# Moving the copy of the transposed attention output from ScalarE to VectorE

## The chip, the cores and the metric

The program runs on one Trainium2 chip, on all 8 of its NeuronCores, one launch for everything. Each core takes half of the query rows of one of four batch entries. The cores exchange nothing. The metric is the device time of the slowest core, in microseconds (us). Engines are named as in the profile: PE is TensorE's matmul, PEld its weight load, DVE is VectorE, ACT is ScalarE, POOL is GpSimd, SP is SyncE.

## The reference

One transformer layer on x of 4 x 2048 x 4096: a layer norm, causal attention with 32 query heads of width 128 that share one key and one value head (with ALiBi position biases), and a quantised linear layer, all added to x.

```python
xn = _layernorm(x, axis=-1)
q = (xn @ Wq).reshape(B, S, 32, 128); kv = xn @ Wkv
k, v = kv[..., :128], kv[..., 128:]
scores = einsum('bqhd,bkd->bhqk', q, k) * 128 ** -0.5 + alibi bias, causal mask
attn = einsum('bhqk,bkd->bqhd', softmax(scores), v)
W = ((w_q - 128).reshape(O, I // 32, 32) * scales[:, :, None]).reshape(O, I)
out = x + attn.reshape(B, S, H) @ Wo + einsum('bsi,oi->bso', xn, W)
```

## The kernel before

The five stages run one after the other on each core.

- Stage A (layer norm): 16 token blocks of 128 are normalised on VectorE and transposed on TensorE; the transposed tiles psA_tr leave PSUM by copies that alternate between ScalarE and VectorE (lines 311 and 316). Keys kt and values vt are computed here.
- Stage B (queries): 64 products of 32 matmuls each (line 411) into qat, which holds 32 heads x 1024 queries, written by ScalarE (line 423).
- Stage C (attention): the stage that the change touches.
- Stage D (output projection): 128 products of 32 matmuls (line 756) that read qat, now the attention output.
- Stage E (quantised layer): dequantisation on VectorE, transposes, matmuls (line 888), sum with x.

**Stage C.** A query pass r (0 or 1) covers 512 queries, and inside a pass the loop runs over the 32 heads. The key blocks (128 keys each) that a head needs are taken in pairs, called groups; the first pass has up to 8 blocks (4 groups), the second up to 16 (8 groups). Blocks whose ALiBi weight is zero are left out, so the first heads have fewer. For one group the work is:

1. two score matmuls of 512 columns into psC_sc (line 524), two slots in PSUM;
2. one exp over 128x1024 on ScalarE into expb (line 551), three slots in SBUF;
3. on VectorE the weights and masks: for heads 0 to 7 ("narrow") small operations per query block (lines 574, 576, 603, some on GpSimd, line 614), for heads 8 to 31 ("wide") only a mask over 128x512 (line 562), and only for four key blocks of the pass: those of groups 0 and 1 in the first pass, of groups 2 and 3 in the second;
4. up to 8 matmuls of 129 columns that multiply with the values into psC_av (line 654). For a wide head the values have been scaled before by vfb (line 506, one operation for each key block).

When a head's groups are done, evA on VectorE takes psC_av out of PSUM (lines 684 and 691). The rest of the head is carried into the next head as `pending`: evB divides by the softmax sums (lines 697 and 706) and writes attn_tm; ctp makes four transposes on TensorE (line 713) into psC_tr, 128x512 in bf16; evat copies psC_tr over the head's queries in qat (line 720). qat is not read again before stage D.

The order is written out by hand. Each engine has its own list of operations, executed in order; semaphores (pe, ve, se, ge: one for each engine) count finished operations. In the loop over groups gi, the score matmuls of group gi are issued ahead of the value matmuls of group gi - 1. ctp and evat of the pending head are issued at gi = min(3, G - 1), right behind the score matmuls of that group and ahead of its exp:

```python
sc_pe = E.op("tensor", smm, wait=waits, inc="pe")          # scores of group gi
if gi == min(3, G - 1) and pending is not None:
    pe_ctp[i_p] = E.op("tensor", pending["ctp"], ...)
    se_evat[i_p] = E.op("scalar", pending["evat"], wait=w, inc="se")
se_exp[it] = E.op("scalar", lambda e, ...: e.activation(..., AF.Exp), ...)
```

evat itself is `e.copy(dst, src) if hasattr(e, "copy") else e.tensor_copy(dst, src)`, so it fits either engine. The last head's evB, ctp and evat are issued by _flush_tail. Below, exp k, mask k, scores k and values k stand for the operations of group k of a head, and "the copy" is evat.

Of the kernel before, what the change touches and what calls it, by code (L numbers as in the profile page):

```python
# [177 lines left out]
def build_nc(debug=DEBUG):  # L178
# [24 lines left out]
    with ExitStack() as stk:  # L203
# [5 lines left out]
        E = Emitter(nc, sems)  # L209
# [40 lines left out]
        for t in range(NT):  # L250
# [4 lines left out]
                wait=[("ve", ve_xn[t - 3] if t >= 3 else 0)], inc=f"ld{t % 3}")  # L255
# [3 lines left out]
            def lnstats(e, b2=b2, b3=b3, c1=c1, c2=c2):  # L259
# [11 lines left out]
                wait=[(f"ld{t % 3}", ld_x[t]), ("ve", ve_xn[t - 2] if t >= 2 else 0)], inc="ve")  # L271
            se_sq = E.op("scalar", lambda e, b2=b2: e.activation(
                lnmv[:, b2 * 4 + 2: b2 * 4 + 3], lnmv[:, b2 * 4 + 1: b2 * 4 + 2], AF.Sqrt),
                wait=[("ve", ve_stats)], inc="se")
            c3 = E.reserve("ve")
            def lnapply(e, b2=b2, b3=b3, c3=c3):
# [7 lines left out]
                wait=[("se", se_sq), ("pe", pe_tpr[t - 2][3] if t >= 2 else 0)], inc="ve")  # L284

            for g in range(4):
# [25 lines left out]
                else:  # L312
                    def evr(e, t=t, g=g, ph_=ph_):
# [5 lines left out]
                                     inc="se" if gid % 2 == 0 else "ve")  # L319

            def vmm(e, t=t):
                ins = None
                for dt in range(32):
                    if t < 8:
                        lhsT = xnt[:, dt * 1024 + t * 128: dt * 1024 + (t + 1) * 128]
                    else:
# [5 lines left out]
                           wait=[("se" if (t * 4 + 3) % 2 == 0 else "ve", seA_evr[t][3]),  # L332
                                 ("se" if (t * 4 + 2) % 2 == 0 else "ve", seA_evr[t][2]),
                                 ("wtc", 48),
                                 ("se", se_evv[t - 1] if t >= 1 else 0)], inc="pe")
            se_evv[t] = E.op("scalar", lambda e, t=t: e.copy(vt[:, t * 129: t * 129 + 128], psA_v[:, 0:128]),
                             wait=[("pe", pe_v[t])], inc="se")

            if t % 4 == 3:
                c = t // 4  # L340
                def kmm(e, c=c):
                    ins = None
                    for dt in range(32):
                        if c < 2:
                            rhs = xnt[:, dt * 1024 + c * 512: dt * 1024 + (c + 1) * 512]
                        else:
# [5 lines left out]
                               wait=[("se", se_evk[c - 1] if c >= 1 else 0)], inc="pe")  # L352
                se_evk[c] = E.op("scalar", lambda e, c=c: e.copy(kt[:, c * 512:(c + 1) * 512], psA_k[:, 0:512]),
                                 wait=[("pe", pe_k[c])], inc="se")
# [5 lines left out]
        if debug:  # L360
            E.op("gpsimd", lambda e: e.dma_start(out=dbg["dbg_kt"], in_=kt[:]),
                 wait=[("se", A_se)], inc="dbg")
            E.op("gpsimd", lambda e: e.dma_start(out=dbg["dbg_vt"], in_=vt[:]),
                 wait=[("se", A_se), ("ge", ge_ones)], inc="dbg")
            E.op("gpsimd", lambda e: e.dma_start(
                out=dbg["dbg_xnt"], in_=xnt[:, 0 * 1024: 1 * 1024]),
                wait=[("se", A_se)], inc="dbg")
# [28 lines left out]
        for p in range(16):  # L396
# [5 lines left out]
                wait=warw, inc=f"wp{p % 2}")  # L402
            for sub in range(2):
                for qc in range(2):
# [13 lines left out]
                    if p == 0 and g == 0:  # L418
# [7 lines left out]
                        wait=[("pe", pe_pang[(p, g)])], inc="se")  # L426
# [3 lines left out]
        if debug:  # L430
            dbg_qt_cnt = E.op("gpsimd", lambda e: e.dma_start(out=dbg["dbg_qt"], in_=qat[:, 0:2048]),
                              wait=[("se", B_se)], inc="dbg")
# [14 lines left out]
        ve_evB = {}  # L447
        pe_ctp = {}
        se_evat = {}
        pending = None  # L450

        def _flush_tail(p):
            i = p["idx"]
            zr_p = E.reserve("ve")
            fn_p = p["evB"]
            ve_evB[i] = E.op("vector", lambda e, fn_p=fn_p, zr_p=zr_p: fn_p(e, zr=zr_p),
                             wait=[("ve", se_evA[i]), ("pe", pe_ctp.get(i - 2, 0))], inc="ve")
            pe_ctp[i] = E.op("tensor", p["ctp"],
                             wait=[("ve", ve_evB[i]), ("se", se_evat.get(i - 2, 0))], inc="pe")
            w = [("pe", pe_ctp[i])]  # L460
            if p["dbg"]:
                w.append(("dbg", dbg_qt_cnt))
            se_evat[i] = E.op("scalar", p["evat"], wait=w, inc="se")

        it_c = 0
        KP = _keepers()
# [2 lines left out]
        for r in range(2):  # L469
            for h in range(NH):  # L470
# [44 lines left out]
                for gi in range(G + 1):  # L515
                    if gi < G:
# [16 lines left out]
                        if gi == 0 and pending is not None:  # L533
                            i_p = pending["idx"]
# [6 lines left out]
                        if gi == min(3, G - 1) and pending is not None:  # L541
                            i_p = pending["idx"]
                            pe_ctp[i_p] = E.op("tensor", pending["ctp"],
                                               wait=[("ve", ve_evB[i_p]),
                                                     ("se", se_evat.get(i_p - 2, 0))], inc="pe")
                            w = [("pe", pe_ctp[i_p])]
                            if pending["dbg"]:
                                w.append(("dbg", dbg_qt_cnt))
                            se_evat[i_p] = E.op("scalar", pending["evat"], wait=w, inc="se")
                            pending = None  # L550
                        se_exp[it] = E.op("scalar", lambda e, slot=slot, eslot=eslot, n=len(grp): e.activation(  # L551
                            expb[:, eslot * 1024: eslot * 1024 + n * 512],
# [1 line left out]
                            wait=[("pe", sc_pe), ("pe", pe_avg.get(it - 3, 0))], inc="se")  # L554
# [451 lines left out]
```

How the kernel before makes its waits and increments, by code:

```python
        def run(e, fn=fn, wait=tuple(wait), inc=inc, inc_n=inc_n, ph=self.phase):  # L160
            with nc.named_scope(ph):
                for s, v in wait:
                    e.wait_ge(sems[s], v)
                ins = fn(e)
                if inc is not None:
                    ins.then_inc(sems[inc], inc_n)
# [92 lines left out]
            def lnstats(e, b2=b2, b3=b3, c1=c1, c2=c2):  # L259
                for c in range(8):
                    ins = e.bn_stats(lnst[:, b2 * 48 + c * 6: b2 * 48 + (c + 1) * 6],
                                     xblk[:, b3 * D + c * 512: b3 * D + (c + 1) * 512])
                ins.then_inc(sems["ve"], 1)
                e.wait_ge(sems["ve"], c1)
                e.bn_aggr(lnag[:, b2 * 2:(b2 + 1) * 2], lnst[:, b2 * 48:(b2 + 1) * 48]).then_inc(sems["ve"], 1)
                e.wait_ge(sems["ve"], c2)
                e.tensor_copy(lnmv[:, b2 * 4: b2 * 4 + 1], lnag[:, b2 * 2: b2 * 2 + 1])
                return e.tensor_scalar(lnmv[:, b2 * 4 + 1: b2 * 4 + 2],
                                       lnag[:, b2 * 2 + 1: b2 * 2 + 2], 1e-5, None, ALU.add)
# [6 lines left out]
            def lnapply(e, b2=b2, b3=b3, c3=c3):  # L276
                e.reciprocal(lnmv[:, b2 * 4 + 3: b2 * 4 + 4],
                             lnmv[:, b2 * 4 + 2: b2 * 4 + 3]).then_inc(sems["ve"], 1)
                e.wait_ge(sems["ve"], c3)
                return e.tensor_scalar(xn_tm[:, b2 * D:(b2 + 1) * D], xblk[:, b3 * D:(b3 + 1) * D],
```

## Time and profile before

| | us |
|---|---|
| median of 2 runs | 2526.25 (2523.46 to 2529.05) |
| the profiled execution | 2525.56 |
| its span, slowest core (cores 2 and 5) | 2524.0 |
| spans of the 8 cores | 2498.8 to 2524.0 |
| mean granted TensorE clock of the cores | 0.880 to 0.898 |
| stage C on core 2, about | 777 to 1485 |

The span is what lies between a core's first and last instruction; the profiled execution's own time is 1.56 us above it. Rows of the profile give the start on the slowest core, the busy time of a group of instructions, and in brackets how long the engine stood idle before it and what released it. Neighbouring instructions of one kind are merged (x8). The granted clock is a fraction of 2.4 GHz; TensorE has the two levels 1.2 and 2.4 GHz, so a mean of 0.65 is a mixture of them.

### The profile page before, as it was taken

What the parts mean: (1) busy time and instruction counts of PE and PEld (TensorE: products, weight loads), DVE (VectorE), ACT (ScalarE), POOL (GpSimd) and SP (SyncE); (2) the same over time, 40 slices, a digit from 0 to 9 for tenths busy, and PEclk for the clock granted to TensorE, in tenths of its full rate; (3) what the DMA queues carried; (4) which work ended last, traced back from release to release, by engine and by line L of the source; (5) the groups of instructions that cost most, each with busy time, mean ns of one, the idle gap of its engine ahead of it and who ended that gap; (6) DMA issues with size and microseconds to landing.
All of it is one profiled execution on the core that took longest, in us unless ns stands there. A gap on an engine that the chain in (4) does not pass through costs nothing.

```text
span 2524.0 us, 39485 instructions; the slowest of 8 cores (2498.8 to 2524.0 us)
## 1 busy us (share of the span) xinstructions
PE 1978.5 (78%) x15451; PEld 1431.1 (57%) x15451; DVE 762.9 (30%) x2024; ACT 571.9 (23%) x659; POOL 87.2 (3%) x103
## 2 busy tenths in 40 slices
PE   1556379999996555666665679999998599999999
PEld 1444234444443333323333358888887488888888
DVE  2666200000003444454434321111111444444442
ACT  0111000000003444445556530000000222222221
POOL 0000000000000000000000000000000000000000
PEclk9666689999996668657989889999999699999999
DMA  7332466676550000005000007788774965555622
GB/s 168 154 143 104 53 71 71 72 84 79 67 67 1 1 1 1 1 1 68 1 1 1 1 5 86 87 100 97 96 88 74 185 166 136 141 142 141 146 82 78
DMA packets 218275, 193.05 MB, mean 76 GB/s; under 512 B 9840, under 2 KB 210544, under 8 KB 211824
## 3 DMA queue, kind: packets, MB, share of 16 engines
q0 software_dynamic: 140736, 103.88, 32.1%
q1 hardware_dynamic: 77360, 86.66, 11.0%
q8 instruction: 128, 2.10, 0.4%
q14 instruction: 51, 0.42, 0.1%
HBM read 269.21 MB, written 25.17 MB: 117 GB/s over the span
## 4 chain that ended last, share of the span: by engine, by line
PE 70%; DVE 12%; ACT 7%; issue 5%; DMA 5%; DVEq 0%; ACTq 0%; POOL 0%; POOLq 0%; SPq 0%
PE psE L888 18%; PE psD L756 18%; PE psD L411 18%; PE psC_av L654 5%; ACT expb L551 5%; PE psC_sc L524 5%; DVE vf L506 3%; DVE lnst L261 2%; PE psE_tr L846 2%; PE psA_tr L299 2%; DMA wkvb<-wkv 2%; DMA wpan<-wq 2%; DVE xn_tm L280 1%; DVE expb L562 1%; DMA scalesb<-scales 1%
## 5 line engine op out<-in xcount | busy, mean ns | idle before, releaser
L888 PE MATMUL psE<-wtp,xnt 128*128 128x256 bf16 x4096 | 468.5, 273 | 22.6 <-ACT wtp L856 22.6
L411 PE MATMUL psD<-xnt,wpan 128*128 128x512 bf16 x2048 | 444.8, 380 | 42.4 <-DMA wpan<-wq 42.4
L756 PE MATMUL psD<-wpan,qat 128*128 128x256 bf16 x4096 | 449.0, 273 | 0.9 <-ACT qat L720 0.9
L888 PEld LDWEIGHTS psE<-wtp,xnt 128*128 128x128 bf16 x4096 | 396.0, 98 | 69.7 <-issue 25.1
L756 PEld LDWEIGHTS psD<-wpan,qat 128*128 128x128 bf16 x4096 | 401.6, 98 | 48.2 <-issue 1.1
L551 ACT ACTIVATE expb<-psC_sc 128x1024 bf16<-128x1024 f32 x333 | 329.2, 1015 | 297.1 <-PE psC_sc L524 296.4
L654 PE MATMUL psC_av<-vf,expb 128*128 128x129 bf16 x1912 | 188.7, 250 | 223.4 <-DVE expb L562 104.9
L411 PEld LDWEIGHTS psD<-xnt,wpan 128*128 128x128 bf16 x2048 | 200.9, 98 | 286.2 <-issue 46.2
L654 PEld LDWEIGHTS psC_av<-vf,expb 128*128 128x128 bf16 x1912 | 146.2, 113 | 323.2 <-issue 317.6
L856 ACT COPY wtp<-psE_tr 128x1024 bf16<-128x1024 bf16 x128 | 129.1, 1012 | 867.7 <-PE psE_tr L846 867.7
L524 PE MATMUL psC_sc<-qat,kt 128*128 128x512 bf16 x659 | 253.4, 492 | 0.8 <-ACT qat L423 0.8
L574 DVE SCALAR_TENSOR_TENSOR expb<-expb,fcols_s,dmask_s 128x128 bf16<-128x128 bf16 x48 | 20.7, 431 | 510.4 <-ACT expb L551 510.4
L767 DVE CAST awo<-psD 128x256 bf16<-128x256 f32 x128 | 54.3, 425 | 396.8 <-PE psD L756 396.8
L299 PE MATMUL psA_tr<-ident_s,xn_tm 128*128 128x128 bf16 x512 | 59.7, 309 | 125.3 <-DVE xn_tm L280 71.6
L820 DVE SCALAR_TENSOR_TENSOR deq<-wqr,scalesb 128x4096 bf16<-128x4096 bf16 x32 | 139.9, 4419 | 34.7 <-DMA scalesb<-scales 34.7
L423 ACT ACTIVATE qat<-psD 128x512 bf16<-128x512 f32 x64 | 38.2, 597 | 448.9 <-PE psD L411 448.9
L900 DVE TENSOR_TENSOR outst<-psE,awin 128x256 f32<-128x256 f32 x128 | 54.1, 423 | 283.7 <-PE psE L888 187.0
L299 PEld LDWEIGHTS psA_tr<-ident_s,xn_tm 128*128 128x128 bf16 x512 | 52.1, 143 | 133.1 <-issue 133.1
L846 PE MATMUL psE_tr<-ident_s,deq 128*128 128x128 bf16 x1024 | 80.1, 223 | 41.2 <-DVE deq L820 39.9
L846 PEld LDWEIGHTS psE_tr<-ident_s,deq 128*128 128x128 bf16 x1024 | 69.3, 100 | 45.3 <-issue 42.3
L562 DVE TENSOR_TENSOR expb<-expb,mwide_s 128x512 bf16<-128x512 bf16 x192 | 70.8, 420 | 79.9 <-ACT expb L551 79.9
L506 DVE TENSOR_SCALAR vf<-vt,fwide_s 128x129 bf16<-128x129 bf16 x550 | 93.7, 252 | 0.0
(49 smaller groups left out, 862.5 us busy)
## 6 DMA issues: line engine op xcount, KB each, us to landing
xblk<-x SPq DMA_DIRECT2D x16, 2048.0 KB, 8.3
wpan<-wq POOLq DMA_DIRECT2D x16, 2048.0 KB, 20.4
wpan<-wo POOLq DMA_DIRECT2D x16, 2048.0 KB, 22.6
wqr<-wqi POOLq DMA_DIRECT2D x32, 1024.0 KB, 10.1
xin<-x SPq DMA_DIRECT2D x128, 128.0 KB, 2.9
out<-outst SPq DMA_DIRECT2D x128, 128.0 KB, 2.2
scr_awo<-awo SPq DMA_DIRECT2D x128, 64.0 KB, 4.9
awin<-scr_awo SPq DMA_DIRECT2D x128, 64.0 KB, 2.5
```

The costliest lines, as they stand in the source:

```text
L299: ins = e.transpose(psA_tr[:, ph_ * 1024 + i * 128: ph_ * 1024 + (i + 1) * 128], xn_tm[:, b2 * D + dt * 128: b2 * D + (dt + 1) * 128], ide ...
L411: ins = e.matmul(psB[:, quarter * 512:(quarter + 1) * 512], wpan[:, bufp * 8192 + dt * 256 + sub * 128: bufp * 8192 + dt * 256 + (sub + 1) ...
L506: ins = e.tensor_scalar(vf[:, bufv * 2064 + ki * 129: bufv * 2064 + (ki + 1) * 129], vt[:, kb * 129: (kb + 1) * 129], fwide[:, ci: ci + 1] ...
L524: ins = e.matmul(psC_sc[:, slot * 1024 + i * 512: slot * 1024 + (i + 1) * 512], kt[:, kb * 128:(kb + 1) * 128], qat[:, h * 1024 + r * 512: ...
L551: se_exp[it] = E.op("scalar", lambda e, slot=slot, eslot=eslot, n=len(grp): e.activation(expb[:, eslot * 1024: eslot * 1024 + n * 512], ps ...
L562: ins = e.tensor_tensor(sl, sl, mwide[:, t * 512:(t + 1) * 512], ALU.mult)
L654: ins = e.matmul(psC_av[:, AVOFF[jj]: AVOFF[jj] + 129], expb[:, slot * 1024 + i * 512 + jj * 128: slot * 1024 + i * 512 + (jj + 1) * 128], ...
L756: ins = e.matmul(psB[:, slot * 512: slot * 512 + 256], qat[:, h * 1024 + qb * 128: h * 1024 + (qb + 1) * 128], wpan[:, bufp * 8192 + h * 2 ...
L820: return e.scalar_tensor_tensor(deq[:, b4 * D:(b4 + 1) * D].rearrange("p (s c) -> p s c", c=32), wqr[:, b4 * D:(b4 + 1) * D].rearrange("p ...
L846: ins = e.transpose(psE_tr[:, ph * 1024 + i * 128: ph * 1024 + (i + 1) * 128], deq[:, b2 * D + it * 128: b2 * D + (it + 1) * 128], ident[:])
L856: return e.copy(dst, src_) if hasattr(e, "copy") else e.tensor_copy(dst, src_)
L888: ins = e.matmul(psE[:, slot * 512: slot * 512 + 256], xnt[:, dt * 1024 + qb * 128: dt * 1024 + (qb + 1) * 128], wtp[:, bufp * 8192 + dt * ...
```

## The change

The copy evat is issued on VectorE in place of ScalarE, in the loop and in _flush_tail. The semaphore that it counts and on which the transposes wait two heads later changes with it, from se to ve. The wait of the copy (for ctp) and its place in the written order stay the same, so it now stands in VectorE's list between the masks of the group ahead and those of its own group.

```diff
@@ _flush_tail
             pe_ctp[i] = E.op("tensor", p["ctp"],
-                             wait=[("ve", ve_evB[i]), ("se", se_evat.get(i - 2, 0))], inc="pe")
+                             wait=[("ve", ve_evB[i]), ("ve", se_evat.get(i - 2, 0))], inc="pe")
...
-            se_evat[i] = E.op("scalar", p["evat"], wait=w, inc="se")
+            se_evat[i] = E.op("vector", p["evat"], wait=w, inc="ve")
@@ loop over groups, gi == min(3, G - 1)
                             pe_ctp[i_p] = E.op("tensor", pending["ctp"],
                                                wait=[("ve", ve_evB[i_p]),
-                                                     ("se", se_evat.get(i_p - 2, 0))], inc="pe")
+                                                     ("ve", se_evat.get(i_p - 2, 0))], inc="pe")
...
-                            se_evat[i_p] = E.op("scalar", pending["evat"], wait=w, inc="se")
+                            se_evat[i_p] = E.op("vector", pending["evat"], wait=w, inc="ve")
```

In the order of instructions, expb holds the exponentials, mwide_s the masks, psC_av the attention sums in PSUM, vf the scaled values, qat the queries and later the attention output. TensorE's list is the same before and after, instruction by instruction.

ScalarE, wide heads of the first pass, before:

```order
L720 COPY qat<-psC_tr 128x512 [waits pe]
L551 ACTIVATE expb<-psC_sc 128x1024 [waits pe] x4
L720 COPY qat<-psC_tr 128x512 [waits pe]
L551 ACTIVATE expb<-psC_sc 128x1024 [waits pe] x4
L720 COPY qat<-psC_tr 128x512 [waits pe]
```

ScalarE at the end of stage C, after (L856 is stage E):

```order
L551 ACTIVATE expb<-psC_sc 128x512 [waits pe]
L551 ACTIVATE expb<-psC_sc 128x1024 [waits pe] x140
L551 ACTIVATE expb<-psC_sc 128x512 [waits pe]
L551 ACTIVATE expb<-psC_sc 128x1024 [waits pe] x159
L856 COPY wtp<-psE_tr 128x8x128 [waits pe] x128
```

Every copy is gone from between the exps.

VectorE, a wide head of the first pass, before: the end of one head's evA, the value scaling, evB, and the four masks, then the next evA.

```order
L691 CAST attn_un<-psC_av 128x256 x2
L506 TENSOR_SCALAR vf<-vt,fwide_s 128x129 [waits ldm,ge,pe]
L506 TENSOR_SCALAR vf<-vt,fwide_s 128x129 x7
L697 RECIPROCAL zz<-zz 128x4 [waits ve,pe]
L706 TENSOR_TENSOR attn_tm<-attn_un,zz 128x256 [waits ve]
L706 TENSOR_TENSOR attn_tm<-attn_un,zz 128x256
L562 TENSOR_TENSOR expb<-expb,mwide_s 128x512 [waits se]
L562 TENSOR_TENSOR expb<-expb,mwide_s 128x512
L562 TENSOR_TENSOR expb<-expb,mwide_s 128x512 [waits se]
L562 TENSOR_TENSOR expb<-expb,mwide_s 128x512
L684 COPY zz<-psC_av 128x2 [waits pe,ve]
```

The same place after:

```order
L706 TENSOR_TENSOR attn_tm<-attn_un,zz 128x256
L562 TENSOR_TENSOR expb<-expb,mwide_s 128x512 [waits se]
L562 TENSOR_TENSOR expb<-expb,mwide_s 128x512
L562 TENSOR_TENSOR expb<-expb,mwide_s 128x512 [waits se]
L562 TENSOR_TENSOR expb<-expb,mwide_s 128x512
L720 COPY qat<-psC_tr 128x512 [waits pe]
L684 COPY zz<-psC_av 128x2 [waits pe,ve]
```

The copy stands behind all masks of the head and ahead of its evA.

VectorE, a wide head of the second pass, after (before, the line L720 is not there and the rest is the same):

```order
L706 TENSOR_TENSOR attn_tm<-attn_un,zz 128x256
L562 TENSOR_TENSOR expb<-expb,mwide_s 128x512 [waits se]
L562 TENSOR_TENSOR expb<-expb,mwide_s 128x512
L720 COPY qat<-psC_tr 128x512 [waits pe]
L562 TENSOR_TENSOR expb<-expb,mwide_s 128x512 [waits se]
L562 TENSOR_TENSOR expb<-expb,mwide_s 128x512
L684 COPY zz<-psC_av 128x2 [waits pe,ve]
```

Here it stands between mask 2 and mask 3.

## Rows read from the trace of the kernel before

**Rows 1.** The page, busy time of the engines over the span.
```profile
PE 1978.5 (78%) x15451; PEld 1431.1 (57%) x15451; DVE 762.9 (30%) x2024; ACT 571.9 (23%) x659; POOL 87.2 (3%) x103
```

**Rows 2.** Busy time by stretch: the two passes of stage C; PEclk, DMA share, GB/s last.
```profile
777.00:1083.00 306.00, 171.80 (x1053) 103.07 (x1070) 140.37 (x592) 135.87 (x155) 7.04 (x16) 0.65 0.00 1
1083.00:1485.00 402.00, 238.72 (x1927) 140.53 (x1962) 174.97 (x777) 225.75 (x243) 8.98 (x16) 0.87 0.10 11
```

**Rows 3.** Waits in stage C, us in total, times, longest.
```profile
ACT expb L551 <- PE psC_sc L524: 268.1, 168, 4.1
...
DVE zz L684 <- PE psC_av L654: 256.6, 64, 6.0
...
ACT qat L720 <- PE psC_tr L713: 54.0, 46, 4.3
```

**Rows 4.** The chain that ended last, end of a wide head, first pass.
```profile
978.64 0.44 PE psC_tr L713 x4
...
979.64 1.04 ACT expb L551
...
980.82 1.04 PE psC_av L654 x8
```

**Rows 5.** Timeline of the same head: start, busy, engine, instruction, idle time before.
```profile
974.58 1.43 DVE L562 TENSOR_TENSOR expb<-expb,mwide_s 128x512 bf16<-128x512 bf16 x4
...
977.58 1.06 PE L524 MATMUL psC_sc<-qat,kt 128*128 128x512 bf16 x2
977.62 1.02 ACT L551 ACTIVATE expb<-psC_sc 128x1024 bf16<-128x1024 f32 x1 [3.32 <-PE psC_sc L524]
...
978.43 0.63 PE L713 MATMUL psC_tr<-ident_s,attn_tm 128*128 128x128 bf16 x4
...
978.86 1.07 PE L654 MATMUL psC_av<-vf,expb 128*128 128x129 bf16 x8
979.16 0.59 ACT L720 COPY qat<-psC_tr 128x512 bf16<-128x512 bf16 x1 [0.52 <-PE psC_tr L713]
...
982.02 0.23 DVE L684 COPY zz<-psC_av 128x2 f32<-128x2 f32 x2 [6.01 <-PE psC_av L654]
```

**Rows 6.** Timeline of a wide head, second pass, TensorE at its high level.
```profile
1444.68 1.02 ACT L551 ACTIVATE expb<-psC_sc 128x1024 bf16<-128x1024 f32 x1 [2.60 <-PE psC_sc L524]
...
1445.04 0.38 PE L524 MATMUL psC_sc<-qat,kt 128*128 128x512 bf16 x1
...
1445.73 0.59 ACT L720 COPY qat<-psC_tr 128x512 bf16<-128x512 bf16 x1
1445.80 0.76 DVE L562 TENSOR_TENSOR expb<-expb,mwide_s 128x512 bf16<-128x512 bf16 x2 [1.63 <-ACT expb L551]
1446.21 1.03 ACT L551 ACTIVATE expb<-psC_sc 128x1024 bf16<-128x1024 f32 x1
...
1447.34 0.76 DVE L562 TENSOR_TENSOR expb<-expb,mwide_s 128x512 bf16<-128x512 bf16 x2 [0.78 <-ACT expb L551]
...
1448.25 0.33 PE L654 MATMUL psC_av<-vf,expb 128*128 128x129 bf16 x3 [0.55 <-DVE expb L562]
...
1449.17 1.03 ACT L551 ACTIVATE expb<-psC_sc 128x1024 bf16<-128x1024 f32 x1 [0.29 <-PE psC_sc L524]
```

**Rows 7.** Timeline of a wide head, second pass, TensorE at its low level.
```profile
1258.98 1.06 PE L524 MATMUL psC_sc<-qat,kt 128*128 128x512 bf16 x2
...
1261.04 1.95 ACT L551 ACTIVATE expb<-psC_sc 128x1024 bf16<-128x1024 f32 x2
...
1262.18 0.76 DVE L562 TENSOR_TENSOR expb<-expb,mwide_s 128x512 bf16<-128x512 bf16 x2 [1.81 <-ACT expb L551]
```

**Rows 8.** The tile psA_tr of stage A: ns min/median/max, first and last start.
```profile
L311 ACT COPY xnt<-psA_tr x16: 1012/1013/1013, 47.2 to 153.3; 128x1024 bf16<-128x1024 bf16 x16
L311 DVE COPY xnt<-psA_tr x16: 691/692/692, 48.1 to 154.1; 128x1024 bf16<-128x1024 bf16 x16
```

**Rows 9.** The tile psC_av, the same columns.
```profile
L684 DVE COPY zz<-psC_av x128: 149/156/161, 783.4 to 1481.1; 128x2 f32<-128x2 f32 x128
```

## The prediction

> **What bounds the kernel now.** I read the page first. TensorE is busy for 78% of the span [rows 1], but this share is a mean over stages: in stages D and E it works nearly without a gap, in stage C it does not. So I split stage C into its two passes with the view by stretch [rows 2]. In the first pass (306 us) TensorE is busy 171.8 us, VectorE 140.4, ScalarE 135.9; in the second (402 us) 238.7, 175.0 and 225.8. No engine is full. Such a stage is bound by a chain of hand-overs, and the list of waits in stage C says which: ScalarE's exps wait 268 us for scores, evA waits 257 us for the last values of a head, and the copy that is to be moved makes ScalarE wait 54 us for the transposes [rows 3]. The last of the three is the question. ScalarE works in order, so while it waits for the transposes and then copies, the exp behind it cannot start, although its scores are there.
>
> The chain of waits shows that this is on the path: for a wide head of the first pass it runs from the transposes over exp 3 to values 3 [rows 4]. The timeline of the same head gives the times [rows 5]: scores 3 end at 978.64 (977.58 + 1.06), the transposes at 979.06, the copy starts at 979.16, exp 3 at 979.64. Values 3 follow at 980.82, and the next head's evA at 982.02.
>
> **What is removed from ScalarE.** Without the copy, exp 3 waits for its scores and for exp 2. Hand-overs in rows 4 and 5 take 0.10 us (transposes to copy) and 0.14 (exp to values); for scores to exp I take 0.16. Then exp 3 starts at 978.64 + 0.16 = 978.80, 0.84 us earlier than now. Exp 2 is no obstacle: two exps in a row take 1.95 us [rows 7], so one follows the other after 0.93, here at 977.62 + 0.93 = 978.55. Values 3 could start at 980.82 - 0.84 = 979.98, and values 2 are out of the way by then (978.86 + 1.07 = 979.93) [rows 5]. So all 0.84 us reach values 3, and from there evA, the value scaling and the masks of the next head.
>
> That holds with TensorE at its low level (1.2 GHz). At the high level (2.4 GHz) the transposes are shorter. In rows 6 scores 3 end at 1445.42, but exp 2, started at 1444.68, lets the next one go only at 1445.61; exp 3 started at 1446.21, so 0.60 us are there to gain.
>
> **What is added to VectorE.** One copy of 128x512 bf16 from PSUM for each of 64 heads. The trace has no such operation on VectorE. Its neighbours are a copy of 128x1024 bf16 from PSUM, 692 ns against ScalarE's 1013 [rows 8], and one of 128x2, 156 ns [rows 9]. These are the two bounds; halfway in columns lies (692 + 156) / 2 = 424 ns, and I take that. It counts only where VectorE has something else to do:
>
> - First pass, wide heads: the four masks run from 974.58 to 976.01 and VectorE then idles until 982.02 [rows 5], because groups 2 and 3 have no mask. The copy would run from about 979.16 to 979.6, or to 979.9 with 692 ns. The next evA comes at 981.2 at the earliest. Cost 0 with either bound.
> - Second pass, wide heads: the copy stands between mask 2 and mask 3. At the high level mask 2 ends at 1446.56 and the transposes are done before that, so VectorE copies from about 1446.48 to 1446.90 (one operation starts some 0.08 before the other's end). Exp 3, started at 1445.61, would free mask 3 at 1446.74. Mask 3 starts at 1446.85 to 1446.9 in place of 1447.34 [rows 6]: about 0.45 earlier, not 0.60.
> - At the low level scores 3 end at 1260.04, exp 3 moves from 1261.04 to 1260.20, and mask 3 from 1262.18 to 1261.34 [rows 7]; the copy, free to start behind the transposes at about 1260.56, is done by 1260.98 or, with the upper bound, 1261.25. Cost 0.
>
> **What of it survives to the end of the head.** In the first pass exp 3 is the last of the head, so all of it does. In the second pass four more groups follow. Exp 4 waits for scores 4, which stand behind values 2 and mask 2 in TensorE's list and do not move. Mask 3 earlier brings values 3, scores 5 and exp 5 earlier; exp 5 then starts right behind exp 4. In the high-level head the rows give some 0.4 us at exp 5 (now 1449.17), and scores 6 behind values 4, which wait for exp 4 and do not move, leave at most 0.3 at the end of the head, perhaps nothing. I take 0.29. In the low-level head exp 4 was itself behind exp 3 (the merged row of two exps from 1261.04 [rows 7]), so values 3, scores 5 and exp 5 move by nearly all of it; I take 0.75 of the 0.84. In two narrow heads of the second pass, which have five groups, exp 4 waits for its scores and nothing survives.
>
> The copy is executed once in each head but the first, 63 times, and once in the tail. I went through all 63 in the timeline; they fall into these groups:
>
> - first pass, narrow: 7 copies, 0.80 us each, 5.6 us. Where a head has three groups the copy stands behind mask 1, not mask 2, with VectorE idle;
> - first pass, wide: 24 copies; 19 at 0.84 or near it, 5 at 0.46 to 0.65 at the high level; 17.7 us;
> - second pass, narrow: 6 copies at 0.79, 4.7 us, and 2 at 0;
> - second pass, wide, at the low level or with fewer groups: 13 copies, 0.75 each, 9.8 us;
> - second pass, wide, at the high level: 11 copies at 0.29, 3.2 us;
> - tail: stage D waits for the last copy, 0.59 - 0.42 = 0.2 us.
>
> The sum is 41 us. Its own low end is 34 (nothing in the 11 high-level heads, two thirds of the 9.8), its high end 48 (all of exp 3's gain reaches the end everywhere). Stages A, B, D and E keep their instructions, and D's first weights are issued from POOL, which this does not touch.
>
> **The clock.** The mean granted clock is 0.65 in the first pass and 0.87 in the second [rows 2], so TensorE is at its low level for 70% and 26% of the time (twice what is missing to 1). If that share falls by a tenth of a pass, its busy work in that tenth takes half as long: 306 x 0.1 x 0.56 / 2 = 8.6 us in the first pass, 402 x 0.1 x 0.59 / 2 = 11.9 in the second. I expect a little: the idle 1 us between values 2 and values 3 closes, so the same work stands in a shorter time. But the long gap at the head's start, in which VectorE does evA, scaling, evB and mask 0, stays. I add 3 us and keep 15 on either side.
>
> The Trainium skill, "TensorE: Matmul & The Clock Gate", section "HAM oscillation — how this bites in real kernels", says that pauses of TensorE between bursts put it back to half rate and each burst then starts slow. The trace agrees that the two levels alternate inside stage C [rows 2]; by this rule alone the direction is the one I took, and the size would be the rival below.
>
> **Forecast.** 2525.56 - 41 - 3 = 2481.6, say 2482 us. The profiled execution is 0.7 us below the median of the runs, so nothing is corrected for that.
>
> **Rivals.**
>
> 1. *The clock rises markedly.* A denser stage C keeps TensorE at its high level for a tenth more in both passes. For it: the levels clearly follow TensorE's work, and spans of cores with the same work differ. Against it: the longest gap is untouched. 2525.6 - 41 - 20.5 = 2464 us.
> 2. *The second pass gives nothing.* The in-order VectorE holds mask 3 back, or exp 3 never was the late one there. For it: VectorE is as busy as that in this pass, and exp 4 hangs on scores 4. Against it: rows 7, where mask 3 waits 1.81 us for exp 3. Only the first pass counts: 2525.6 - 23.3 = 2502 us.
> 3. *Slower: the copy holds VectorE's list.* Behind it stand mask 3, evA, the next head's scaling. If the transposes come so late that the copy cannot start before mask 3 started until now, mask 3 is late by the copy. It decides at 1447.34 - 0.42 = 1446.9 for the end of the transposes in rows 6; they end before 1445.73 now, so they would have to be 1.2 us later. Price: up to 0.61 us (the upper bound of the copy less the overlap) in the 32 heads of the second pass, 19.5 us, and with no gain in the first pass 2525.6 + 19.5 = 2545 us.
> 4. *Nothing changes*, because exp 3 is held by something else: 2525. Against it stands the chain, which goes through it.
>
> The page "VectorE: DVE Perf Modes" of the Trainium skill, section "Rules for kernel authors", speaks for rival 3: it says to accept one element per cycle on a matmul's output, and by its section on the errata a PSUM copy then costs 120 + 512 cycles at 0.96 GHz, an estimate of 658 ns; it also places VectorE nearer to SBUF and ScalarE nearer to PSUM. The trace does not agree: 1024 columns in 692 ns [rows 8] are more than one for each cycle, and VectorE is the faster of the two. With 658 ns mask 3 of rows 6 would start 0.28 us earlier than now, so the 11 high-level heads would keep nearly the same; it is rival 3 that such a copy would make likelier.
>
> **Chances.** Forecast 0.70, rival 1 0.15, rival 2 0.10, rival 3 0.03, rival 4 0.02. The range that holds 8 in 10 takes the sum from 34 to 48 and the clock by 15 either way: 2525.6 - 48 - 15 = 2463 at the low end, 2525.6 - 34 + 15 = 2507 at the high one. Two per cent, about what a measurement of this kernel can tell from no change, is 50.5 us, so faster begins below 2476. That is rival 1 and the lucky fifth of the forecast's own spread: 0.30. Slower by that much needs 2577, beyond rival 3: 0.01. The rest is 0.69.
>
> **What would show it.** Right: exp 3 starts 0.16 us behind its scores or 0.93 behind exp 2 in every head; from one evA to the next a low-level wide head of the first pass is 0.84 us shorter, and a high-level one of the second pass about 0.3; the copy takes 0.42 us on VectorE; ScalarE's busy time falls by 64 x 0.59 = 38 us [rows 5] and VectorE's rises by 27; the granted clock of the first pass is at or a little above 0.65. Wrong: high-level heads of the second pass of the old length, and low-level ones too (rival 2); a mean clock that moves by more than 0.05 in either pass, which would outweigh a third of the sum; a wait of mask 3 or evA for the copy (rival 3).

## The result, and the profile after

The changed kernel takes 2493.9 us (median of 11 runs) against 2530.4 us (median of 10); the ratio is 0.986, with a 95% interval of 0.983 to 0.990. So it is 1.4% faster, some 35 us, which is inside the 2% that I had called no change. Ratios here and below leave out executions in which the cores of one die were held at a lower clock; the medians do not, so between kernels the ratios are compared. The profiled execution took 2495.26 us, 30.3 us less than that of before.

The page of after, first the busy times:

```profile
PE 1959.3 (79%) x15451; PEld 1419.6 (57%) x15451; DVE 787.2 (32%) x2088; ACT 538.7 (22%) x595; POOL 87.0 (3%) x103
...
L756 PE MATMUL psD<-wpan,qat 128*128 128x256 bf16 x4096 | 451.1, 274 | 6.8 <-DMA wpan<-wo 5.9
```

Against [rows 1] ScalarE has lost 33 us and VectorE has gained 24. The second line is stage D on this core (core 6): it waited 5.9 us for its weights (wpan<-wo). Core 2, the one of [rows 1], had no such wait; core 6 of the kernel before had one of 3.4 us.

The waits in stage C of after (engine, line, what it waited for: us in total, times, longest):

```profile
ACT expb L551 <- PE psC_sc L524: 332.5, 215, 3.7
DVE zz L684 <- PE psC_av L654: 159.8, 63, 6.2
...
DVE qat L720 <- PE psC_tr L713: 77.0, 43, 3.2
```

Against [rows 3]: the wait for the transposes has moved from ScalarE to VectorE, where it replaces idle time that evA had spent waiting for values (257 to 160 us). ScalarE now waits for scores, and for 4.6 us in all for values (psC_av).

The tile psC_tr of after (ns min/median/max, first and last start):

```profile
L720 DVE COPY qat<-psC_tr x64: 409/424/426, 786.0 to 1445.1; 128x512 bf16<-128x512 bf16 x64
```

The timeline of a wide head in the first pass, after, as in [rows 5]:

```profile
869.57 0.23 DVE L684 COPY zz<-psC_av 128x2 f32<-128x2 f32 x2 [1.35 <-PE psC_av L654]
...
872.63 1.43 DVE L562 TENSOR_TENSOR expb<-expb,mwide_s 128x512 bf16<-128x512 bf16 x4
...
875.63 1.06 PE L524 MATMUL psC_sc<-qat,kt 128*128 128x512 bf16 x2
...
876.48 0.63 PE L713 MATMUL psC_tr<-ident_s,attn_tm 128*128 128x128 bf16 x4
...
876.84 1.02 ACT L551 ACTIVATE expb<-psC_sc 128x1024 bf16<-128x1024 f32 x1 [0.15 <-PE psC_sc L524]
876.91 2.12 PE L654 MATMUL psC_av<-vf,expb 128*128 128x129 bf16 x16
877.22 0.42 DVE L720 COPY qat<-psC_tr 128x512 bf16<-128x512 bf16 x1 [3.17 <-PE psC_tr L713]
...
879.21 0.23 DVE L684 COPY zz<-psC_av 128x2 f32<-128x2 f32 x2 [1.56 <-PE psC_av L654]
```

Scores 3 end at 876.69 and exp 3 starts 0.15 us later, beside the transposes; values 2 and 3 are one row of 16 matmuls without a pause; the copy ends at 877.64 and VectorE then still waits 1.56 us for evA. From evA to evA this low-level head takes 879.21 - 869.57 = 9.64 us. The head of [rows 5], whose evA is at 982.02, began with this one:

```profile
971.52 0.23 DVE L684 COPY zz<-psC_av 128x2 f32<-128x2 f32 x2 [6.01 <-PE psC_av L654]
```

It took 10.50 us (other heads of its kind 10.49), so a low-level head has lost 0.85 to 0.86 us. The wide heads of the first pass at the high level went from 8.68 to 8.19 us.

And the second pass at the high level, as in [rows 6] (two exps merged into one row):

```profile
1304.88 1.94 ACT L551 ACTIVATE expb<-psC_sc 128x1024 bf16<-128x1024 f32 x2 [2.60 <-PE psC_sc L524]
...
1306.00 0.76 DVE L562 TENSOR_TENSOR expb<-expb,mwide_s 128x512 bf16<-128x512 bf16 x2 [1.63 <-ACT expb L551]
1306.68 0.42 DVE L720 COPY qat<-psC_tr 128x512 bf16<-128x512 bf16 x1
...
1307.01 0.75 DVE L562 TENSOR_TENSOR expb<-expb,mwide_s 128x512 bf16<-128x512 bf16 x2
...
1313.30 0.23 DVE L684 COPY zz<-psC_av 128x2 f32<-128x2 f32 x2 [5.53 <-PE psC_av L654]
```

From mask 2 to mask 3 it is 1.01 us, where it was 1.54; VectorE goes from mask 2 to the copy to mask 3 without a pause.

The slowest core alone mixes stages and cores, so I measured all eight. The passes are taken from the first evA to that of head 31, and from there to the last; the clocks are the granted clocks in the same stretches. Means over the 8 cores, in us (the second profiles of both kernels, taken on two different chips, are in the last two columns):

| | before | after | before again | after again |
|---|---|---|---|---|
| first pass (clock) | 294.8 (0.70) | 268.6 (0.74) | 296.0 (0.68) | 267.3 (0.75) |
| second pass (clock) | 403.6 (0.85) | 390.3 (0.84) | 405.6 (0.85) | 390.2 (0.84) |
| TensorE busy, first pass | 163.4 | 157.3 | 166.9 | 155.7 |
| TensorE busy, second pass | 246.2 | 250.4 | 248.3 | 250.3 |
| last matmul of B to first of D | 710.7 | 670.7 | 713.9 | 669.3 |
| D, first to last matmul | 449.8 | 451.1 | 452.2 | 452.4 |
| from there to the last matmul of E | 581.7 | 586.0 | 582.8 | 584.4 |

Stage C has lost 40.0 us, with the cores closer together (before 702.8 to 721.2, after 668.1 to 672.7). TensorE executes the same instructions in all four profiles, so its busy time shows the clock: it worked faster in the first pass after the change and a little slower in the second. The span from slowest core to slowest core adds up: core 2 before against core 6 after has -2.2 us up to the end of stage B, -37.3 in stage C, +7.9 in D and +1.3 from there to the end of E, which makes -30.3.

### The profile page after: what moved, and what is told of

It is laid out like the page before. It is cut to its first block, busy times and chain, and to the rows that moved or that the text cites. A ratio compares the mean times of both kernels' runs of the same rounds, so it can differ in the third digit from the quotient of the medians.

```text
span 2493.7 us, 39485 instructions; the slowest of 8 cores (2475.2 to 2493.7 us)
## 1 busy us (share of the span) xinstructions
PE 1959.3 (79%) x15451; PEld 1419.6 (57%) x15451; DVE 787.2 (32%) x2088; ACT 538.7 (22%) x595; POOL 87.0 (3%) x103
## 4 chain that ended last, share of the span: by engine, by line
PE 66%; DVE 13%; DMA 9%; ACT 6%; issue 5%; DVEq 0%; ACTq 0%; POOL 0%; SPq 0%; POOLq 0%
PE psD L411 18%; PE psE L888 17%; PE psD L756 15%; PE psC_av L654 6%; PE psC_sc L524 5%; ACT expb L551 5%; DMA wpan<-wo 4%; DVE vf L506 3%; DVE lnst L261 2%; PE psE_tr L846 2%; PE psA_tr L299 2%; DMA wkvb<-wkv 2%; DMA wpan<-wq 2%; DMA scalesb<-scales 1%; DVE xn_tm L280 1%
## 5 line engine op out<-in xcount | busy, mean ns | idle before, releaser
L756 PE MATMUL psD<-wpan,qat 128*128 128x256 bf16 x4096 | 451.1, 274 | 6.8 <-DMA wpan<-wo 5.9
L551 ACT ACTIVATE expb<-psC_sc 128x1024 bf16<-128x1024 f32 x333 | 326.9, 1013 | 338.3 <-PE psC_sc L524 332.5
L856 ACT COPY wtp<-psE_tr 128x1024 bf16<-128x1024 bf16 x128 | 129.0, 1012 | 891.6 <-PE psE_tr L846 891.6
L654 PEld LDWEIGHTS psC_av<-vf,expb 128*128 128x128 bf16 x1912 | 142.4, 111 | 294.8 <-issue 290.4
L524 PE MATMUL psC_sc<-qat,kt 128*128 128x512 bf16 x659 | 242.6, 474 | 0.8 <-ACT qat L423 0.8
```

The source lines that it names most:

```text
L524: ins = e.matmul(psC_sc[:, slot * 1024 + i * 512: slot * 1024 + (i + 1) * 512], kt[:, kb * 128:(kb + 1) * 128], qat[:, h * 1024 + r * 512: ...
L654: ins = e.matmul(psC_av[:, AVOFF[jj]: AVOFF[jj] + 129], expb[:, slot * 1024 + i * 512 + jj * 128: slot * 1024 + i * 512 + (jj + 1) * 128], ...
L756: ins = e.matmul(psB[:, slot * 512: slot * 512 + 256], qat[:, h * 1024 + qb * 128: h * 1024 + (qb + 1) * 128], wpan[:, bufp * 8192 + h * 2 ...
L856: return e.copy(dst, src_) if hasattr(e, "copy") else e.tensor_copy(dst, src_)
```

## The experiments

Theory A: the gain is that the exp no longer stands behind the transposes and the copy. Theory B, a rival: it is that the copy is shorter on VectorE. Others came up on the way: C on TensorE's clock, D on stage D's weights.

**e1: the copy stays on ScalarE, behind the exp of its group.**

```diff
-                            se_evat[i_p] = E.op("scalar", pending["evat"], wait=w, inc="se")
...
                         se_exp[it] = E.op("scalar", lambda e, ...: e.activation(...), ...)
+                        if late is not None:
+                            se_evat[late[0]] = E.op("scalar", late[1], wait=late[2], inc="se")
```

> The copy stays on ScalarE and is issued behind the exp of its group instead of ahead of it. If the gain is that the exp no longer stands behind the transposes and the copy (theory A), stage C gets shorter by about 40 us as with the change, and the time is 2490 us (2482 to 2500), since the copy then runs in ScalarE's idle time; in the second pass exp 4 could be late by up to 0.2 us a head, 5 us in all. If the gain is that VectorE copies faster than ScalarE (0.42 against 0.59 us, theory B), there is none here: 2526 us.

Measured: 2495.3 us, ratio 0.983 (0.976 to 0.990); first pass 268.6, second 390.7 us. The timeline of ScalarE on core 6 shows the new order, exp 2, exp 3, copy:

```profile
961.33 1.02 ACT L552 ACTIVATE expb<-psC_sc 128x1024 bf16<-128x1024 f32 x1 [3.12 <-PE psC_sc L525]
962.50 1.02 ACT L552 ACTIVATE expb<-psC_sc 128x1024 bf16<-128x1024 f32 x1 [0.15 <-PE psC_sc L525]
963.43 0.58 ACT L724 COPY qat<-psC_tr 128x512 bf16<-128x512 bf16 x1
```

The passes are those of the change to 0.4 us, with the copy still on ScalarE and as long as ever (0.58 us). Theory B falls.

**e2 and e3: the copies of one pass only on VectorE.** The edit makes engine and semaphore depend on the copy's number (below: e2; e3 turns the condition round).

```diff
+        def ev_eng(i):
+            return "vector" if i < NH - 1 else "scalar"
...
-                            se_evat[i_p] = E.op("vector", pending["evat"], wait=w, inc="ve")
+                            se_evat[i_p] = E.op(ev_eng(i_p), pending["evat"], wait=w, inc=ev_sem(i_p))
```

> The copies issued in the first pass (31 of 64) go to VectorE, the others stay on ScalarE. From the traces of before and after (means over the 8 cores: first pass 294.8 to 268.6 us, second 403.6 to 390.3) theory A expects the first pass at 269 us, the second at 403, and a time of 2501 us (2494 to 2508). If a pass influenced the other through the clock, the second pass would not be at 403 but 5 us or more away.

> The reverse: 33 copies (second pass and tail) on VectorE, those of the first pass on ScalarE. Theory A: first pass 295 us, second 390, time 2514 us (2507 to 2521). If VectorE's list holds mask 3 back (rival 2 of the prediction), no gain: 2526 us.

Measured: e2 2502.1 us, ratio 0.986 (0.982 to 0.991), passes 268.1 and 401.4 us; e3 2517.7 us, ratio 0.9955 (0.992 to 0.999), passes 294.3 and 389.1 us. Each pass has the length that goes with the place of its own copies, whatever the other does. Rival 2 of the prediction falls with e3: the second pass does gain.

**e4 and e4_again: one more copy on VectorE.**

```diff
-                    return e.copy(dst_, src_) if hasattr(e, "copy") else e.tensor_copy(dst_, src_)
+                    e.tensor_copy(awo[:, half * 512:(half + 1) * 512], src_)
+                    return e.tensor_copy(dst_, src_)
```

> The changed kernel with a second copy on VectorE, of the same 128x512 from psC_tr into a tile of stage D that is free at that time, ahead of the real one; the result is the same. It prices VectorE's time. Theory A: nothing in the first pass (VectorE idle there, 269 us as with the change), and up to 0.35 us for each of some 24 wide heads in the second, so 390 to 398 us; time 2494 to 2503 us. If VectorE's list is the bound in both passes, each pass grows by 0.35 us a head, 11 us each: 2516 us.

Measured: 2486.5 us in the profiled execution, ratio 0.981 (0.974 to 0.989), an interval that overlaps the change's own; first pass 268.6 us, second 385.3 us, at a clock of 0.87. The first pass is as long as expected, but by two effects: its seven narrow heads, in which masks stand behind the copies, take 56.3 us where they took 54.3 (0.3 us a head), and its 24 wide heads 212.3 where they took 214.3. The second went the other way, 5.0 us shorter than with the change, though more work stands on VectorE. All eight cores together show where it is: six of them need 382.0 to 384.4 us at a clock of 0.88 to 0.90, the other two 391.3 and 393.1 at 0.83. This is where theory C comes from: the lengths of the heads (from evA to evA) in the second pass take few values. With the change a high-level head takes 13.37 us, and after one to three of them, once four, comes a run of about five of 14 to 15 us in which TensorE is at its low level for a time. With one more copy it takes 13.56 us, and up to 13 (one of 13.84 among them) follow each other before a drop. Before, it took 13.77 us, in runs of up to six. Of the last 18 heads of the pass 4.6 on a core have the high-level length with the change, 9.8 with one more copy, and 7.6 before. So a head that moves by 0.2 us goes together with another number of drops, and one drop costs some 4 to 5 us (14.98, 13.98, 14.08, 14.48 and 14.52 us in place of five times 13.56 is 4.2).

> The kernel with one additional copy once more. If its short second pass is the kernel's own, the mean over the cores is 383 to 387 us and most cores show heads of 13.56 us in runs of ten or more, with a granted clock near 0.87. If it was one execution's luck, the second pass is at 390 us and the clock at 0.84.

Measured: 2493.5 us in one run; first pass 267.7, second 386.4 us, clock 0.87; six cores again with heads of 13.56 us in long runs (383.2 to 384.2 us on five of them, 388.6 on core 2), two at 391.4. The evA rows of VectorE show a run and a drop, on core 4 here:

```profile
1313.15 0.22 DVE L684 COPY zz<-psC_av 128x2 f32<-128x2 f32 x2 [5.39 <-PE psC_av L654]
1326.71 0.23 DVE L684 COPY zz<-psC_av 128x2 f32<-128x2 f32 x2 [5.39 <-PE psC_av L654]
1340.27 0.23 DVE L684 COPY zz<-psC_av 128x2 f32<-128x2 f32 x2 [5.39 <-PE psC_av L654]
1353.82 0.23 DVE L684 COPY zz<-psC_av 128x2 f32<-128x2 f32 x2 [5.39 <-PE psC_av L654]
1368.80 0.23 DVE L684 COPY zz<-psC_av 128x2 f32<-128x2 f32 x2 [5.59 <-PE psC_av L654]
1382.78 0.23 DVE L684 COPY zz<-psC_av 128x2 f32<-128x2 f32 x2 [5.58 <-PE psC_av L654]
```

Read the differences of the starts: 13.56 three times, then 14.98 and 13.98. The changed kernel, core 0, in the same stretch:

```profile
1339.78 0.23 DVE L684 COPY zz<-psC_av 128x2 f32<-128x2 f32 x2 [5.39 <-PE psC_av L654]
1353.16 0.23 DVE L684 COPY zz<-psC_av 128x2 f32<-128x2 f32 x2 [5.53 <-PE psC_av L654]
1368.14 0.23 DVE L684 COPY zz<-psC_av 128x2 f32<-128x2 f32 x2 [5.60 <-PE psC_av L654]
1382.08 0.23 DVE L684 COPY zz<-psC_av 128x2 f32<-128x2 f32 x2 [5.50 <-PE psC_av L654]
1396.20 0.23 DVE L684 COPY zz<-psC_av 128x2 f32<-128x2 f32 x2 [5.39 <-PE psC_av L654]
```

One head of 13.38, then 14.98, 13.94, 14.12.

**e7b: two more copies.** The same edit with both halves of the unused tile as targets. (An earlier run, e7_vector_thrice, has an expectation for three copies, but its kernel is that of e6; it is told below as a second run of e6, and its expectation was not tested by it.)

> Three copies on VectorE in place of one (two of them additional, into a tile of stage D that is free at that time). One additional copy had made the high-level wide head of the second pass 13.56 us long against 13.37, and the second pass 385.3 us against 390.3, by longer unbroken runs of high-level heads. Theory C (the clock decides, with the longest runs near 13.6 us): with 13.9 us a head the runs are short again, the second pass is at 395 us or more, its granted clock at 0.85 or less. If an additional copy helps in itself, the second pass is at 386 us or less. First pass 267 to 269 us by either, VectorE being idle there.

Measured: 2498.2 us in one run; first pass 271.2, second 394.7 us, clock 0.85. The high-level head takes 13.89 us and the longest run of them is three. So the second pass goes 390, 385 or 386, 395 us with no, one and two more copies: not monotonic, as theory C has it, though 394.7 is 0.3 us short of the number that I had set. No run sets the length of a head and nothing else, so that the length decides is argued; e1, e5 and e6, which leave the copy in three different places and all have high-level heads of 13.37 us, speak for it with second passes of 390.4 to 391.5 us. Why 13.56 us keeps the high level longer than 13.37 stays open. The first pass was expected at 267 to 269 and is 2 us above it. That is in its narrow heads again: 54.3, 56.3 and 58.4 us with no, one and two more copies, while the wide heads have 214.3, 212.3 and 212.8 us. In the narrow heads VectorE's time in front of the weights and masks is not free. One place of the kind, on core 7, with the two extra copies (awo), the real one, and the weights behind them:

```profile
821.51 0.58 DVE L576 TENSOR_SCALAR expb<-expb,fcols_s 128x128 bf16<-128x128 bf16 x3 [2.88 <-ACT expb L551]
822.00 0.42 DVE L720 COPY awo<-psC_tr 128x512 bf16<-128x512 bf16 x1
822.34 0.41 DVE L721 COPY awo<-psC_tr 128x512 bf16<-128x512 bf16 x1
822.67 0.41 DVE L722 COPY qat<-psC_tr 128x512 bf16<-128x512 bf16 x1
823.00 0.57 DVE L576 TENSOR_SCALAR expb<-expb,fcols_s 128x128 bf16<-128x128 bf16 x3
```

**e5: the copy on VectorE, behind the mask of its group.**

```diff
-                            se_evat[i_p] = E.op("vector", pending["evat"], wait=w, inc="ve")
...
+                    if late is not None:
+                        se_evat[late[0]] = E.op("vector", late[1], wait=late[2], inc="ve")
+                        late = None
                     if gi >= 1:
```

> The copy on VectorE, but issued behind the mask of its group (behind mask 3), so that it can't hold a mask back. First pass 268.6 us as with the change. By the hand-overs a high-level wide head of the second pass would be 0.12 us shorter than the 13.37 us of the change. If such time is simply saved, the second pass is at 387 to 390 us and the time 2490 us. If the granted clock decides more than that (theory C: long unbroken runs of high-level heads come with heads of about 13.6 us, and a head farther from that drops to the low level oftener), the second pass is at 390 to 396 us although less work stands in the way.

Measured: 2496.2 us, ratio 0.985 (0.979 to 0.990); passes 267.0 and 390.6 us; the high-level head 13.37 us, the same as with the change. The 0.12 us at mask 3 is not on the path to the end of the head, so this run does not tell the two expectations apart.

**e6: no copy in the loop.** Stage D then reads the queries in place of the attention output of all heads but the last one of the second pass, whose copy is in the tail.

```diff
-                            se_evat[i_p] = E.op("scalar", pending["evat"], wait=w, inc="se")
```

> Before without the 63 copies of the loop (the attention output is left out of what stage D reads, which reads the queries in its place; the transposes stay). It takes the copy off both engines. Theory A: first pass 268 to 269 us, the same as with the copy on VectorE or behind the exp, so that the copy costs nothing there wherever it stands out of the exps' way; second pass 386 to 392 us. If VectorE's copy had a price, it would be missing here: first pass 258 us or less.

Measured: 2495.6 us in the profiled execution; first pass 268.0, second 391.5 us. The second run of the same file, whose expectation was written for three copies, gave 267.9 and 390.4 us:

> Two copies on VectorE in addition to the real one, where the run with one in addition had a second pass of 385.3 us (mean of the cores) against 390.3 with none. Theory C: a high-level head becomes some 13.9 us long, runs of unbroken high-level heads get short again, and the second pass is at 395 us or more, though one more copy had made it shorter. If an additional copy helps in itself, the second pass is at 385 us or less. First pass 268 to 270 us by either.

With no copy on any engine the passes are those of the change (268.6 and 390.3) and of e1 (268.6 and 390.7). This is the plainest answer: the copy costs nothing that these passes show where it stands now, neither on VectorE nor behind the exp on ScalarE. All that could be gained in stage C by getting the copy out of the way has been gained.

**after_again and before_again: second profiles.**

> The changed kernel once more, for a second profile. If the pass lengths are the kernel's and not one execution's, first pass 268.6 and second 390.3 us within 1.5 us (means of the 8 cores). If pairs of cores that begin stage D within some 4 us of each other share a source of weights (theory D), their stage D takes 451 us or more on one of them, and 448 to 450 on the cores of other pairs.

> The kernel before once more, for a second profile to hold against the second one of the changed kernel. First pass 294.8 and second 403.6 us within 2 us (means of the cores). From the last matmul of stage D to the last of stage E 581.7 us before and 586.0 and 584.4 in the two profiles of the change: if the change itself gives that back, this one is at 583 or less; if it is chance, it may be at 584 to 587. Cores of one pair that begin stage D within some 4 us of each other: one of them needs 451 us or more for it, the others 448 to 450 (theory D).

The runs took 2493.0 us (after again) and 2545.9 us (before again). The passes are in the table above: after again 267.3 and 390.2 us, within the 1.5 us expected; before again 296.0 and 405.6, within 2 us. So the gain in the passes is 26.2 and 13.3 us by the first profiles, 28.6 and 15.4 by the second. From the end of D to the end of E it is 581.7 and 582.8 us before, 586.0 and 584.4 after; the kernels e1 to e9, which have the same stage E, lie between 581.7 and 584.5. So 2 to 3 us may be given back behind stage C, but this is no more than these kernels differ among themselves, and I leave it open.

Theory D had more to stand on. In 14 profiles there are 56 pairs of cores (0 and 1, 2 and 3, and so on). Starts are counted on each core from its own first instruction, so "within" supposes that the two cores of a pair begin their spans together, which the profile does not show. In the 22 pairs that began stage D within 2.8 us of each other, the slower core of the two took 451.0 to 461.6 us for it; in the 30 pairs that were 4.2 us or more apart, no core took more than 450.3. The four pairs between have 450.4 to 451.8. In all 22 close pairs the slower core is the one that began later, and it has waited 1.3 us or more for the weights wpan; no core of a far pair has waited more than 0.3. Nearness to a core of another pair does nothing: of the 60 cores whose partner was far, 42 had such a core within 2.8 us, and none of them took more than 450.3. It is not the change's doing: the longest of all is in the unchanged kernel (core 6 in before_again, 461.6 us, started 1.4 us from core 7). The waits in stage D of before_again on core 6:

```profile
PE psD L756 <- DMA wpan<-wo: 9.0, 2, 6.5
PE psD L756 <- ACT qat L720: 0.9, 1, 0.9
```

It looks as if the weights came late to the second of two cores that ask for them at once. This is a correlation over all profiles; no run set the distance between two cores on purpose, so the cause is argued, not shown. It fits core 6 being the slowest of the changed kernel: it began 1.2 us from core 7 and took 457.0 us, 5.9 of the excess being the wait for weights on the page.

**e9: the next head's value scaling ahead of evA.** Stage C being a chain, what stands between evA and the next head's first values is worth moving. VectorE waits there for the last values of a head anyway.

```diff
+                    vfd[nidx] = E.op("vector", vfb, wait=vfw, inc="ve")   # values of head idx + 1
                 def evA(e, bufa=bufa):
...
-                    ve_vf = E.op("vector", vfb, wait=vfw, inc="ve")       # at the head's start
+                ve_vf = vfd.get(idx0, 0)
```

> The changed kernel, and the value scaling of the next head (line 506) issued on VectorE ahead of evA in place of behind it, where VectorE waits for the last values of a head. The chain from evA to the next head's first values then loses the scaling: 1.3 us a wide head in the first pass (24 heads, 30 us), and in the second up to 2.6 us (24 heads), of which I expect two thirds, 40 us. First pass 240 us, second 350 us; the time 2424 us (2405 to 2450) if theory A's picture of stage C as one chain of hand-overs is right. If stage C is bound by an engine's work instead, no more than 10 us.

Measured: 2402.1 us, ratio 0.948 (0.946 to 0.951): 5.2% faster than before. First pass 232.4 us (clock 0.80), second 330.4 (clock 0.91), stage C 574.6 us. VectorE on core 7:

```profile
1248.39 0.76 DVE L548 TENSOR_TENSOR expb<-expb,mwide_s 128x512 bf16<-128x512 bf16 x2 [2.01 <-ACT expb L537]
1249.07 0.42 DVE L724 COPY qat<-psC_tr 128x512 bf16<-128x512 bf16 x1
1249.40 0.75 DVE L548 TENSOR_TENSOR expb<-expb,mwide_s 128x512 bf16<-128x512 bf16 x2
1250.07 2.69 DVE L676 TENSOR_SCALAR vf<-vt,fwide_s 128x129 bf16<-128x129 bf16 x16
1255.68 0.23 DVE L688 COPY zz<-psC_av 128x2 f32<-128x2 f32 x2 [2.92 <-PE psC_av L640]
```

The 16 scalings now run before evA, and VectorE still waits 2.92 us there. The time lies below the 2405 to 2450 expected: the high-level head takes 11.41 us, and on all eight cores none of the last 19 heads is longer than 11.69; the granted clock of this stretch is 1.00, where it was 0.90 with the change. The hand-overs alone would have given 13.37 - 2.6 = 10.8 us for such a head at best, and with two thirds of the 2.6 us, as expected, 11.6; so the head came out near the expectation. The second pass lies 20 us below the expected 350, and most of this goes with the clock: with the change 13 of its last 18 heads on a core were not at the high level, at 1.1 us each.

## Why the prediction was right

I had forecast 2482 us, range 2463 to 2507, and no change beyond 2% as the likeliest class. The median is 2493.9 and the ratio says 35 us where I had said 44. Step by step:

- *ScalarE is released, exp 3 starts 0.84 us earlier at the low level and 0.60 at the high.* Right. Exp 3 follows its scores after 0.15 us in the timeline after, the low-level wide head of the first pass is 0.85 us shorter, and e1 and e6 show that the exp's release is the whole of the gain in stage C. ScalarE's busy time fell by 33 us and not 38, VectorE's rose by 24 and not 27: busy time counts overlaps once, and neighbours overlap (the copy of [rows 6] ends at 1446.32, the exp behind it starts at 1446.21).
- *The copy takes 424 ns on VectorE.* The median is 424. The point halfway between 128x2 and 128x1024 held. The estimate of 658 ns, worked out from the page "VectorE: DVE Perf Modes" of the Trainium skill (sections "Rules for kernel authors" and "The TRN2 errata"), did not.
- *It costs nothing in the first pass, and mask 3 of the second starts 0.45 us earlier.* Right; by the rows it is 1.54 - 1.01 = 0.53 us. Even this was not on the path (e5).
- *First pass 23.3 us.* Measured 26.2 and 28.6. The seven narrow heads lost 5.6 us, as forecast, the wide ones 20.6 and 22.9 where I had 17.7. The excess goes with the clock, 0.70 to 0.74 and 0.68 to 0.75. (My own terms were loose here: 19 times 0.84 and 5 times 0.46 to 0.65 make 18.3 to 19.2, not 17.7.)
- *Second pass 17.7 us, of which 0.29 us in each high-level head.* The head was mis-sized: it lost 0.40 us (13.77 to 13.37), more than I had given it. But the pass gave only 13.3 and 15.4 us, because fewer heads were at the high level: of its last 18 heads 7.6 and 6.6 on a core before, 4.6 and 4.9 after, and each that is not costs 1.1 us more (14.5 against 13.37), some 2 to 3 us in all.
- *Clock: 3 us in all, from less idle time.* This is the step that failed in its form. I had treated the clock as something that rises where the same work stands closer. In the first pass it did, and by more than I had allowed: by 0.04 and 0.07, where I had set a move of more than 0.05 in either pass as a sign of being wrong. In the second pass it fell a little (0.85 to 0.84), as the heads of 13.37 us came in shorter runs than those of 13.77; e4 and e7b, which add work to the head, move the same pass by -5 and +4 us. The sum over both passes, 41 + 3, met 40.0 and 44.6 partly by the luck of opposite signs.
- *Stages D and E are untouched.* Right in their instructions. But I had not asked when the cores of a pair arrive at stage D, and the slowest core of the profile after is one that arrived just behind its partner. The mean of the cores has 40.0 us less in stage C, the slowest core 30.3 us less in all; of the difference 7.9 us is in its stage D. That this belongs to the change is not shown: the cores reached stage D over 25.0 and 18.2 us before and 7.2 and 12.6 after, but over 25.2 us in e1, which has the same stage C.

Rival 1 (clock up in both passes) came in the first pass alone: a tenth more time at the high level is 0.05 in the mean clock, which is what the two pairs of profiles show, and the pass gave 3 to 5 us beyond the forecast, not the 8.6 that I had priced. Rival 2 fell with e3, rival 3 with the rows of both passes and e6, rival 4 with the passes.

## What to carry to other kernels

An engine that executes its list in order holds back everything behind an instruction that waits: look for an instruction whose wait ends later than that of the one queued behind it, and move either the instruction or its place. Which of the two did not matter here, as e1 shows. Then ask what else stands between the end of one round and the start of the next on an engine that idles just before: here that took another 96 us off stage C (e9, 670.7 to 574.6). And compare kernels of this kind by the means over cores and by stage, since the slowest core adds its own clock and its own wait for weights.

## What I had not expected of the hardware

- More work can go with a shorter stage. With one more copy of 0.42 us per head the second pass was 4 to 5 us shorter on average (390.3 and 390.2 to 385.3 and 386.4 us), with the granted clock up from 0.84 to 0.87; with two more it was 4.4 us longer. High-level heads came in long runs at 13.56 us, in shorter ones at 13.37, 13.77 and 13.89, and without a break at 11.41. What decides this is open.
- Where two cores of a pair begin stage D, and with it the reading of its weights, within 2.8 us of each other, the later one is slow: 451.0 to 461.6 us in 22 of 22 cases, against 450.3 at most in 30 of 30 pairs that were 4.2 us or more apart.
- VectorE copies 128x1024 and 128x512 bf16 out of PSUM faster (692 and 424 ns) than ScalarE (1013 and 587).
